# Decoder on one core: two of eight multiplications per expert tile moved from VectorE to ScalarE and GpSimd

## The chip, the cores and the metric

The kernel runs on one core of a Trainium2 chip. The metric is the device time of one execution in microseconds (us), over several runs of the same program. A core has TensorE (matmuls, PE in the profile; its weight loads are PEld), VectorE (DVE), ScalarE (ACT), GpSimd (POOL) and SyncE (SP). Each engine works through its own instruction list in order; semaphores tie the lists together.

## The reference

Two decoder layers over 16 x 256 tokens of width 256: causal attention, cross attention and a product-key expert layer (PEER), then banded attention, a BiDAF-like mix and a mixture of experts. Only the PEER layer is touched:

```python
q = (x @ Wq + bq).reshape(B, S, N_HEADS, D_QUERY)
s1 = einsum('bshd,nd->bshn', q1, K1); s2 = einsum('bshd,nd->bshn', q2, K2)
v1, i1 = top_k(s1, 10); v2, i2 = top_k(s2, 10)
vals, best = top_k(all pair sums, 10)
expert_idx = take_along_axis(i1 * 64 + i2, best)
scores = softmax(vals)
h = einsum('bsd,bshkd->bshk', x, W_down[expert_idx])
h = gelu(h) * scores
out = einsum('bshk,bshkd->bsd', h, W_up[expert_idx])
```

## The kernel before

The stages run one after another. `peer_stage` does 32 tiles of 128 tokens. It gathers nothing: all 4096 experts (32 groups `v` of 128) are computed densely, and a matrix of routing weights, zero where a token did not choose an expert, is multiplied in. A tile `t` is cut into eight chunks `n` of 16 tokens for the routing weights, and into eight quarters of four expert groups for the activations.

What one turn of the tile loop does on each engine, chunk by chunk (`macro` of each engine, in this order; nothing reorders it at run time):

- TensorE: `weights(t, n)` (L1000) makes the routing weights of 16 tokens with 48 small matmuls from one-hot matrices into one of two PSUM banks, `ps_w[:, n % 2]`. Called w(n) below. Between w(n) and w(n+1) stand `output(t-1)` (L1009, four expert groups of the tile before, from `g` and `up`) and `hidden(t+1)` (L990, the activations of four groups of the next tile into `ps_h`): out(n-1) and hid(n-1). For tile t+2, `turn_x` (L964) comes after w(1), `queries` (L971) after w(2), `scores` (L981) after w(3); `turn_uvw(t+1)` (L1018) comes after hid(4). Ahead of w(n), TensorE waits until the bank has been read, that is until the product of chunk n-2 is done.
- VectorE: for each n, `hots` (L1233, L1237) builds one-hot matrices two chunks ahead (`hot_e`, `hot_u`), then `weigh(n-1)` (L1245) multiplies `ps_w` into the 128x512 slice of `g`. The rest of the list is the choice of experts for later tiles: `best_eight`, `next_eight`, `places`, `lookup`, `choices` for t+1 and `halves` (L1258 to L1276) for t+2. The choice for t+1 ends in `uvw`, which TensorE turns (`turn_uvw`) and ScalarE takes (`take_uvw`, L1107 to L1109, semaphore `uvw_used`); `hots(t+1, 0)` at n = 6 waits for that.
- ScalarE: `gelu(t+1, n-1)` (L1087) after each hid(n-1), reading `ps_h` and writing `g`; at n = 1, 2, 3 it takes `xnT`, `qT` and `s` for tile t+2; at n = 2 `take_code`; at n = 3, behind `gelu(t+1, 2)`, `exps(t+1)` (L1093: a table load and eight small activations), at n = 5 `take_uvw`.
- GpSimd: `norm` (L1161) and `candidates` (L1175) at the tile's head, then `hots` (L1190): three 80x512 products `hot_v` from `hot_e` per chunk, two chunks ahead; `split` (L1154 to L1157) before those of chunk 0.

Of the kernel before, what the change touches and what calls it, by code (L numbers as in the profile page):

```python
# [6 lines left out]
P = 128  # L7
ALU = mybir.AluOpType
# [44 lines left out]
class Room:  # L53
# [12 lines left out]
    def sb(self, name, shape, dt=F32):  # L66
        return self.ctx.enter_context(self.nc.sbuf_tensor(f"{self.stage}_{name}", shape, dt))
# [4 lines left out]
    def sem(self, name):  # L72
        self.sems.append(self.nc.alloc_semaphore(f"{self.stage}_{name}"))
        return self.sems[-1]
# [751 lines left out]
EV = 32  # L826
CHUNK = 16
# [12 lines left out]
def peer_stage(nc, stats, ident, d):  # L840
# [6 lines left out]
    with ExitStack() as ctx:  # L847
        r = Room(nc, ctx, "peer")
        stats.open(r)
        sb, ps, sem = r.sb, r.ps, r.sem  # L850
        SEL = NQ * TOP
        wq = sb("wq", [P, DC, 2 * NQ * HALF])
        bq = sb("bq", [P, 4])
        keys = sb("keys", [P, 2 * KEYS])
# [33 lines left out]
        hot_v = sb("hot_v", [P, RING, 3, CHUNK // 2, EV, 2], BF16)  # L888
        g = sb("g", [P, 2, EV, P])
        mark = sb("mark", [P, 1])  # L890

        ps_q = ps("ps_q", [P, 512])
        ps_s = ps("ps_s", [P, 2, 512])
# [26 lines left out]
        v_ready = sem("v_ready")  # L920
        w_done = sem("w_done")
        gw_ready = sem("gw_ready")
        up_done = sem("up_done")
        x_used = sem("x_used")
        roots_ready = sem("roots_ready")
# [20 lines left out]
        def there(t):  # L946

            return not isinstance(t, int) or 0 <= t < TILES

        def by_pair(row, n):  # L950

# [3 lines left out]
        def _(pe):  # L955
# [38 lines left out]
            def weights(t, n):  # L994
                pe.wait_ge(u_ready, NCH * t + n + 1)
                pe.wait_ge(v_ready, NCH * t + n + 1)
                wait(pe, gw_ready, NCH * t + n - 1)
                for k in range(CHUNK):
                    for part in range(3):
                        mm = nc.tensor.matmul(ps_w[:, n % 2, k * EV:(k + 1) * EV], hot_u[0:SEL, n % RING, k // 2, :, k % 2],  # L1000
                                              hot_v[0:SEL, n % RING, part, k // 2, :, k % 2], start=(part == 0), stop=(part == 2))
                mm.then_inc(w_done, 1)

            def output(t, par, a, b):
                if a == 0:
                    pe.wait_ge(gw_ready, NCH * (t + 1))
                    wait(pe, x_used, t)
                for v in range(a, b):
                    mm = nc.tensor.matmul(ps_u[:], g[:, par, v, :], up[:, v, :], start=(v == 0), stop=(v == EV - 1))  # L1009
                if b == EV:  # L1010
                    mm.then_inc(up_done, 1)
# [51 lines left out]
        def _(act):  # L1063
# [20 lines left out]
            def gelu(t, par, n):  # L1084
# [2 lines left out]
                nc.scalar.activation(g[:, par, 4 * n:4 * n + 4, :].rearrange("p v s -> p (v s)"), ps_h[:, n % 2, :],  # L1087
                                     ACT.Gelu).then_inc(g_ready, 1)

            def exps(t):  # L1090
                act.wait_ge(exp_in, t + 1)
                for h in range(NQ):
                    ins = nc.scalar.activation(ew[:, h, :], ew[:, h, :], ACT.Exp, accum_out=es[:, h, :])  # L1093
                ins.then_inc(exp_out, 1)
# [28 lines left out]
            def macro(t, par):  # L1123
                for n in range(NCH):
                    if there(t + 2):
                        if n == 1:
                            take_x(t + 2, par)
                        if n == 2:
                            take_q(t + 2)
                        if n == 3:  # L1130
                            take_s(t + 2)
                    if there(t + 1):
                        if n == 2:
                            take_code(t + 1)
                        if n > 0:
                            gelu(t + 1, 1 - par, n - 1)
                        if n == 3:
                            exps(t + 1)
                        if n == 5:
                            take_uvw(t + 1, 1 - par)  # L1140
                if there(t + 1):
                    gelu(t + 1, 1 - par, NCH - 1)

# [3 lines left out]
        def _(pool):  # L1147
# [35 lines left out]
            def hots(t, par, n):  # L1183
# [6 lines left out]
                    ins = nc.gpsimd.tensor_tensor(hot_v[0:SEL, n % RING, part], hot_e[0:SEL, n % RING], w, ALU.mult)  # L1190
                ins.then_inc(v_ready, 1)

            def first():
                pool.wait_ge(roots_ready, 1)
                norm(0)
                norm(1)
                candidates(0)
                for n in range(AHEAD):
                    hots(0, 0, n)

            def macro(t, par):
                if there(t + 2):
                    norm(t + 2)
                if there(t + 1):
                    candidates(t + 1)
                for n in range(NCH):
                    if n < NCH - AHEAD:
                        hots(t, par, n + AHEAD)
                    elif there(t + 1):
                        hots(t + 1, 1 - par, n + AHEAD - NCH)  # L1210
                    if n == AGAIN:
                        steps.again()

# [3 lines left out]
        def _(dve):  # L1217
# [22 lines left out]
            def weigh(t, par, n):  # L1240
                if n == 0:
                    dve.wait_ge(g_ready, NCH * (t + 1))
                dve.wait_ge(w_done, NCH * t + n + 1)
                gs = g[:, par, :, n * CHUNK:(n + 1) * CHUNK]
                nc.vector.tensor_tensor(gs, ps_w[:, n % 2, :].rearrange("p (k v) -> p v k", v=EV), gs,  # L1245
                                        ALU.mult).then_inc(gw_ready, 1)
# [1059 lines left out]
```

## Time and profile before

| | us |
|---|---|
| three runs | 3786.21, 3789.82, 3791.73 (median 3789.82) |
| profiled execution, device time | 3788.22 |
| its span | 3786.4 |
| PEER stage, first to last product of `weigh` | 982.4 to 2473.6 |

| engine | busy of the span | busy of one steady PEER tile (47.41 us) |
|---|---|---|
| PE | 3288.4 (87%) | 44.00 |
| DVE | 2719.1 (72%) | 46.19 |
| ACT | 1203.2 (32%) | 12.61 |
| POOL | 2068.0 (55%) | 36.23 |

The profiled execution is 1.6 us below the median. A steady tile lasts from one `turn_x` to the next; the 28 that follow each other from 1030 to 2358 us are 47.1 to 47.6 us long. Busy shares are a mean over stages with different limits, so the last column is what counts for a change inside PEER. An engine's position in its instruction list matters too: it can be idle in one place of the tile and late in another.

### The profile page before, as it was taken

The numbers are of one execution on the slowest core, as the hardware profiler recorded it, in microseconds if no ns is written. First come the engines' busy times: TensorE is split into PE (matmuls) and PEld (weight loads), VectorE is DVE, ScalarE is ACT, GpSimd is POOL, SyncE is SP. The second block draws the span as 40 slices with busy tenths as digits, with TensorE's granted clock in tenths as the row PEclk, the third lists the DMA queues.
The fourth block names the chain that finished last, engine by engine and source line by source line (L and its number), as shares of the span: only waits on it lengthen the run. The fifth ranks groups of instructions, "written<-read, shape, count | busy, mean of one in ns | idle before, by whom it ended". The sixth has DMA issues, their size and how long they took to land. (4 is left out here: it accounts for less than half of the span.)

```text
span 3786.4 us, 93267 instructions
## 1 busy us (share of the span) xinstructions
PE 3288.4 (87%) x33694; PEld 2790.3 (74%) x33695; DVE 2719.1 (72%) x10688; ACT 1203.2 (32%) x3140; POOL 2068.0 (55%) x2392
## 2 busy tenths in 40 slices
PE   6999957786599999999999999978888897699998
PEld 4777735554488888888888888855564687699998
DVE  6666634554999999999999999948887554533333
ACT  1443435552222222222222222225664221122221
POOL 4444335551677777777777777858885000233333
PEclk8999978997799999999999999989999896799999
DMA  5444434443000000000000000034453115466665
GB/s 152 110 108 110 109 83 116 123 113 122 1 2 2 2 2 2 2 2 2 2 2 2 2 2 2 2 91 124 125 130 74 34 33 160 123 181 183 182 182 136
DMA packets 256114, 277.90 MB, mean 73 GB/s; under 512 B 44001, under 2 KB 200673, under 8 KB 255201
## 3 DMA queue, kind: packets, MB, share of 16 engines
q1 hardware_dynamic: 242081, 253.69, 23.5%
q0 software_dynamic: 13632, 18.91, 3.3%
q8 instruction: 245, 4.01, 0.4%
q14 instruction: 156, 1.28, 0.1%
HBM read 187.63 MB, written 72.29 MB: 69 GB/s over the span
## 5 line engine op out<-in xcount | busy, mean ns | idle before, releaser
L1190 POOL TENSOR_TENSOR peer_hot_v<-peer_hot_e,peer_parts 80x512 bf16<-80x512 bf16 x768 | 990.9, 1316 | 320.9 <-DVE peer_hot_e L1233 311.7
L1009 PE MATMUL peer_ps_u<-peer_up,peer_g 128*128 128x256 f32 x2048 | 534.3, 408 | 0.6 <-DVE x_all L1331 0.6
L990 PEld LDWEIGHTS peer_ps_h<-peer_xnT,peer_down 128*128 128x128 f32 x4096 | 512.7, 197 | 15.7 <-DMA peer_down<-in_peer_down 0.9
L990 PE MATMUL peer_ps_h<-peer_xnT,peer_down 128*128 128x128 f32 x4096 | 512.3, 280 | 0.6 <-DMA peer_down<-in_peer_down 0.6
L1000 PE MATMUL peer_ps_w<-peer_hot_v,peer_hot_u 80*128 80x32 bf16 x12288 | 347.3, 177 | 145.4 <-DVE peer_g L1245 97.5
L1000 PEld LDWEIGHTS peer_ps_w<-peer_hot_v,peer_hot_u 80*128 80x128 bf16 x12288 | 337.0, 97 | 167.3 <-issue 92.1
L1009 PEld LDWEIGHTS peer_ps_u<-peer_up,peer_g 128*128 128x128 f32 x2048 | 393.1, 202 | 53.5 <-issue 1.0
L1087 ACT ACTIVATE peer_g<-peer_ps_h 128x512 f32<-128x512 f32 x256 | 152.9, 597 | 840.5 <-PE peer_ps_h L990 840.2
L1237 DVE TENSOR_TENSOR peer_hot_u<-peer_count,peer_uvT 80x2048 bf16<-80x2048 bf16 x256 | 349.4, 1365 | 0.0
L2072 POOL DMA_INDIRECT out<-moe_y,moe_target x71 | 112.6, 1585 | 312.6 <-DVE moe_y L2203 309.6
L2007 PE MATMUL moe_ps_t<-moe_xgT,moe_w 128*128 128x128 f32 x2272 | 267.3, 276 | 0.0
L2066 POOL DMA_INDIRECT moe_xg<-moe_xn_rows,moe_source x71 | 70.2, 988 | 357.2 <-DVE moe_target L2173 325.0
L2007 PEld LDWEIGHTS moe_ps_t<-moe_xgT,moe_w 128*128 128x128 f32 x2272 | 261.5, 193 | 0.1
L2017 PE MATMUL moe_ps_y<-moe_w,moe_hT 128*128 x1136 | 256.8, 379 | 0.0
L2017 PEld LDWEIGHTS moe_ps_y<-moe_w,moe_hT 128*128 128x128 f32 x1136 | 210.5, 190 | 25.7
L772 DVE TENSOR_REDUCE band_nmax<-band_ps 128x2 f32<-128x512 f32 x256 | 171.3, 680 | 42.4 <-PE band_ps L511 42.1
L769 DVE TENSOR_REDUCE causal_nmax<-causal_ps 128x1 f32<-128x128 f32 (+1 forms) x512 | 153.2, 349 | 58.1 <-PE causal_ps L515 57.7
L634 ACT ACTIVATE causal_probT<-causal_ps 128x384 f32<-128x384 f32 x256 | 124.7, 489 | 202.4 <-PE causal_ps L538 199.4
L1245 DVE TENSOR_TENSOR peer_g<-peer_ps_w,peer_g 128x512 f32<-128x512 f32 x256 | 173.8, 679 | 7.4 <-PE peer_ps_w L1000 7.4
L2203 DVE SCALAR_TENSOR_TENSOR moe_y<-moe_ps_y,moe_gate,moe_b2w 128x256 f32<-128x256 f32 x71 | 34.4, 484 | 194.9 <-PE moe_ps_y L2017 194.9
L634 ACT ACTIVATE band_probT<-band_ps 128x512 f32<-128x512 f32 x256 | 147.2, 594 | 62.1 <-PE band_ps L535 57.7
L772 DVE TENSOR_REDUCE cross_nmax<-cross_ps 128x2 f32<-128x240 f32 x256 | 97.8, 400 | 96.0 <-PE cross_ps L511 95.0
(362 smaller groups left out, 7073.9 us busy)
## 6 DMA issues: line engine op xcount, KB each, us to landing
moe_w<-in_moe_w SPq DMA_DIRECT2D x142, 512.0 KB
causal_qs<-causal_qscratch SPq DMA_DIRECT2D x32, 384.0 KB, 3.9
cross_qs<-cross_qscratch SPq DMA_DIRECT2D x32, 384.0 KB, 3.6
band_qs<-band_qscratch SPq DMA_DIRECT2D x32, 384.0 KB, 4.1
moe_w<-in_moe_w SPq DMA_DIRECT2D x8, 1024.0 KB, 11.7
causal_qscratch<-causal_part SPq DMA_DIRECT2D x32, 192.0 KB, 2.6
causal_kscratch<-causal_part SPq DMA_DIRECT2D x32, 192.0 KB, 2.0
causal_ks<-causal_kscratch SPq DMA_DIRECT2D x32, 192.0 KB, 4.2
```

The source lines that it names most:

```text
L634: nc.scalar.activation(probT[0:KN, h, :], ps_2[0:KN, h % 2, 0:COLS], ACT.Exp).then_inc(p_ready, 1)
L769: ins = nc.vector.tensor_reduce(nmax[:, q, h:h + 1], ps_1[:, h % 2, qcol[q]:qcol[q] + seen[q]], AX.X, ALU.max, negate=True)
L772: ins = nc.vector.tensor_reduce(nmax[:, :, h], ps_1[:, h % 2, 0:TT * KS].rearrange("p (q k) -> p q k", q=TT), AX.X, ALU.max, negate=True)
L990: mm = nc.tensor.matmul(ps_h[:, n % 2, k * P:(k + 1) * P], down[:, c, 4 * n + k, :], xnT[:, par, c, :], start=(c == 0), stop=(c == DC - 1))
L1000: mm = nc.tensor.matmul(ps_w[:, n % 2, k * EV:(k + 1) * EV], hot_u[0:SEL, n % RING, k // 2, :, k % 2], hot_v[0:SEL, n % RING, part, k // 2 ...
L1009: mm = nc.tensor.matmul(ps_u[:], g[:, par, v, :], up[:, v, :], start=(v == 0), stop=(v == EV - 1))
L1087: nc.scalar.activation(g[:, par, 4 * n:4 * n + 4, :].rearrange("p v s -> p (v s)"), ps_h[:, n % 2, :], ACT.Gelu).then_inc(g_ready, 1)
L1190: ins = nc.gpsimd.tensor_tensor(hot_v[0:SEL, n % RING, part], hot_e[0:SEL, n % RING], w, ALU.mult)
L1237: nc.vector.tensor_tensor(hot_u[0:SEL, n % RING], numbers.broadcast_to((SEL, CHUNK // 2, P, 2)), ut, ALU.is_equal).then_inc(u_ready, 1)
L1245: nc.vector.tensor_tensor(gs, ps_w[:, n % 2, :].rearrange("p (k v) -> p v k", v=EV), gs, ALU.mult).then_inc(gw_ready, 1)
L2007: mm = nc.tensor.matmul(ps_h[:, half, m * P:(m + 1) * P], w1[:, par, half, c, m * P:(m + 1) * P], xgT[:, par, c, :], start=(c == 0), stop= ...
L2017: mm = nc.tensor.matmul(ps_y[:, par, 0:D], hT[:, par, m, :], w2[:, ex, m, :], start=(m == 0), stop=(m == HC - 1))
```

## The change

Chunks 2 and 5 of each tile (`APART`) are no longer multiplied by VectorE. ScalarE copies the bank `ps_w[:, n % 2]` into a new SBUF buffer `wcopy` (`take_w`, one 128x512 activation), and GpSimd multiplies `wcopy` into the slice of `g` (its own `weigh`, one 128x512 `tensor_tensor`, that reads `wcopy` at a stride of 32 elements). Two semaphores are new: `w_copied` (ScalarE's copy has been made) and `gp_ready` (GpSimd's product has been made). TensorE's wait ahead of w(n) is now `w_free`: for n = 4 and n = 7 on `w_copied`, else on `gw_ready`, whose count is six per tile. `output` waits for both kinds of products before its first matmul of a tile.

```diff
+        APART = (2, 5)
+        HERE = NCH - len(APART)
...
+        def w_free(eng, t, n):
+            if n < 0:
+                t, n = t - 1, n + NCH
+            if t < 0:
+                return
+            if n in APART:
+                eng.wait_ge(w_copied, len(APART) * t + APART.index(n) + 1)
+            else:
+                eng.wait_ge(gw_ready, HERE * t + n + 1 - sum(k < n for k in APART))
...
             def weights(t, n):
-                wait(pe, gw_ready, NCH * t + n - 1)
+                w_free(pe, t, n - 2)
...
             def output(t, par, a, b):
                 if a == 0:
-                    pe.wait_ge(gw_ready, NCH * (t + 1))
+                    pe.wait_ge(gw_ready, HERE * (t + 1))
+                    pe.wait_ge(gp_ready, len(APART) * (t + 1))
...
+            def take_w(t, n):                                  # ScalarE
+                k = APART.index(n)
+                act.wait_ge(w_done, NCH * t + n + 1)
+                wait(act, gp_ready, len(APART) * (t - 1) + k + 1)
+                nc.scalar.activation(wcopy[:, k, :], ps_w[:, n % 2, :], ACT.Copy).then_inc(w_copied, 1)
...
                         if n == 5:
                             take_uvw(t + 1, 1 - par)
+                    if n - 1 in APART:
+                        take_w(t, n - 1)
...
+            def weigh(t, par, n):                              # GpSimd
+                k = APART.index(n)
+                pool.wait_ge(w_copied, len(APART) * t + k + 1)
+                gs = g[:, par, :, n * CHUNK:(n + 1) * CHUNK]
+                nc.gpsimd.tensor_tensor(gs, wcopy[:, k, :].rearrange("p (k v) -> p v k", v=EV), gs, ALU.mult).then_inc(gp_ready, 1)
...
                     elif there(t + 1):
                         hots(t + 1, 1 - par, n + AHEAD - NCH)
+                    if n - 2 in APART:
+                        weigh(t, par, n - 2)
...
             def weigh(t, par, n):                              # VectorE
                 if n == 0:
                     dve.wait_ge(g_ready, NCH * (t + 1))
+                if n in APART:
+                    return
```

ScalarE's list in a steady tile before, from `s` of tile t+2 to the last `gelu` but one. `peer_g<-peer_ps_h` is a `gelu`, `peer_ew` are the exponentials:

```order
L1081 ACTIVATE peer_s<-peer_ps_s 128x1024
L1087 ACTIVATE peer_g<-peer_ps_h 128x512
L1093 ACT_TABLE_LOAD
L1093 ACTIVATE peer_ew,peer_es<-peer_ew 128x10 x8
L1087 ACT_TABLE_LOAD
L1087 ACTIVATE peer_g<-peer_ps_h 128x512 x2
L1107 ACTIVATE peer_uvT<-peer_ps_q 80x256
L1108 ACTIVATE peer_parts<-peer_ps_q 80x128
L1109 ACTIVATE peer_wT<-peer_ps_q 80x128
L1087 ACTIVATE peer_g<-peer_ps_h 128x512 x3
```

The same piece of ScalarE's list in the changed kernel, with the copies as `peer_wcopy`:

```order
L1098 ACTIVATE peer_s<-peer_ps_s 128x1024
L1104 ACTIVATE peer_g<-peer_ps_h 128x512
L1116 ACT_TABLE_LOAD
L1116 ACTIVATE peer_ew,peer_es<-peer_ew 128x10 x8
L1111 ACTIVATE peer_wcopy<-peer_ps_w 128x512
L1104 ACT_TABLE_LOAD
L1104 ACTIVATE peer_g<-peer_ps_h 128x512 x2
L1130 ACTIVATE peer_uvT<-peer_ps_q 80x256
L1131 ACTIVATE peer_parts<-peer_ps_q 80x128
L1132 ACTIVATE peer_wT<-peer_ps_q 80x128
L1104 ACTIVATE peer_g<-peer_ps_h 128x512
L1111 ACTIVATE peer_wcopy<-peer_ps_w 128x512
```

The copy of chunk 2 stands behind the exponentials and ahead of the second table load; that of chunk 5 stands behind `gelu(t+1, 5)`.

GpSimd's list before, from the `hot_v` products of a tile to the head of the next:

```order
L1190 TENSOR_TENSOR peer_hot_v<-peer_hot_e,peer_parts 80x512 x9
L1154 TENSOR_TENSOR peer_rest<-peer_wT,peer_parts 80x128
L1155 CAST peer_parts<-peer_rest 80x128
L1156 TENSOR_TENSOR peer_rest<-peer_rest,peer_parts 80x128
L1157 CAST peer_parts<-peer_rest 80x128
L1190 TENSOR_TENSOR peer_hot_v<-peer_hot_e,peer_parts 80x512 x6
L1161 TENSOR_SCALAR peer_xn<-x_all,mean,rstd 128x256
```

The same piece in the changed kernel:

```order
L1215 TENSOR_TENSOR peer_hot_v<-peer_hot_e,peer_parts 80x512 x6
L1222 TENSOR_TENSOR peer_g<-peer_wcopy,peer_g 128x32x16
L1215 TENSOR_TENSOR peer_hot_v<-peer_hot_e,peer_parts 80x512 x3
L1179 TENSOR_TENSOR peer_rest<-peer_wT,peer_parts 80x128
L1180 CAST peer_parts<-peer_rest 80x128
L1181 TENSOR_TENSOR peer_rest<-peer_rest,peer_parts 80x128
L1182 CAST peer_parts<-peer_rest 80x128
L1215 TENSOR_TENSOR peer_hot_v<-peer_hot_e,peer_parts 80x512 x6
L1222 TENSOR_TENSOR peer_g<-peer_wcopy,peer_g 128x32x16
L1186 TENSOR_SCALAR peer_xn<-x_all,mean,rstd 128x256
```

The product of chunk 2 stands between the `hot_v` of chunks 6 and 7, that of chunk 5 between the `hot_v` of the next tile's chunk 1 and `norm`. On TensorE no instruction moves, only what w(4) and w(7) wait for; on VectorE the products of chunks 2 and 5 are gone and nothing else moves.

## Rows read from the trace of the kernel before

**Rows 1.** Windows: us, busy (count) of PE, PEld, DVE, ACT, POOL; PEclk; DMA

```profile
1741.58:1788.99 47.41, 44.00 (x620) 41.13 (x616) 46.19 (x235) 12.61 (x36) 36.23 (x35) 0.97 0.01 2
1030.00:2358.00 1328.00, 1226.44 (x17155) 1148.99 (x17151) 1293.82 (x6552) 353.16 (x1008) 1018.31 (x954) 0.97 0.01 2
1741.40:1744.80 3.40, 3.40 (x22) 2.86 (x19) 3.40 (x4) 0.38 (x1) 3.40 (x3) 0.50 0.00 0
```

**Rows 2.** Timeline of PE in one steady tile: start, us, group

```profile
1740.37 1.37 PE L1000 MATMUL peer_ps_w<-peer_hot_v,peer_hot_u 80*128 80x32 bf16 x48 [0.96 <-DVE peer_g L1245]
...
1742.04 3.27 PE L1009 MATMUL peer_ps_u<-peer_up,peer_g 128*128 128x256 f32 x8
1745.14 1.95 PE L990 MATMUL peer_ps_h<-peer_xnT,peer_down 128*128 128x128 f32 x16
...
1750.00 1.89 PE L1009 MATMUL peer_ps_u<-peer_up,peer_g 128*128 128x256 f32 x8
1751.73 1.95 PE L990 MATMUL peer_ps_h<-peer_xnT,peer_down 128*128 128x128 f32 x16
...
1757.72 1.95 PE L990 MATMUL peer_ps_h<-peer_xnT,peer_down 128*128 128x128 f32 x16
1759.50 1.36 PE L1000 MATMUL peer_ps_w<-peer_hot_v,peer_hot_u 80*128 80x32 bf16 x48
...
1765.71 1.35 PE L1000 MATMUL peer_ps_w<-peer_hot_v,peer_hot_u 80*128 80x32 bf16 x48 [1.24 <-DVE peer_g L1245]
...
1770.50 0.49 PE L1018 MATMUL peer_ps_q<-ident,peer_uvw 128*80 128x128 f32 x3
1771.22 1.35 PE L1000 MATMUL peer_ps_w<-peer_hot_v,peer_hot_u 80*128 80x32 bf16 x48 [0.23 <-DVE peer_g L1245]
...
1774.23 1.95 PE L990 MATMUL peer_ps_h<-peer_xnT,peer_down 128*128 128x128 f32 x16
1777.16 1.35 PE L1000 MATMUL peer_ps_w<-peer_hot_v,peer_hot_u 80*128 80x32 bf16 x48 [0.98 <-DVE peer_g L1245]
...
1787.79 1.35 PE L1000 MATMUL peer_ps_w<-peer_hot_v,peer_hot_u 80*128 80x32 bf16 x48 [0.96 <-DVE peer_g L1245]
```

**Rows 3.** Timeline of ACT in the same tile

```profile
1759.70 0.60 ACT L1087 ACTIVATE peer_g<-peer_ps_h 128x512 f32<-128x512 f32 x1 [2.67 <-PE peer_ps_h L990]
1760.32 1.28 ACT L1093 ACT_TABLE_LOAD   x1
...
1763.08 0.19 ACT L1093 ACTIVATION_READ_ACCUMULATOR peer_ew<-peer_ew 128x1 f32 x1
...
1771.62 0.28 ACT L1109 ACTIVATE peer_wT<-peer_ps_q 80x128 f32<-80x128 f32 x1
```

**Rows 4.** Timeline of DVE in the same tile

```profile
1757.07 0.68 DVE L1245 TENSOR_TENSOR peer_g<-peer_ps_w,peer_g 128x512 f32<-128x512 f32 x1
1757.69 0.06 DVE L1258 MEMSET peer_mark<- 128x1 f32 x1
...
1774.86 0.42 DVE L1233 TENSOR_TENSOR peer_hot_e<-peer_count,peer_uvT 80x512 bf16<-80x512 bf16 x1
...
1786.96 0.68 DVE L1245 TENSOR_TENSOR peer_g<-peer_ps_w,peer_g 128x512 f32<-128x512 f32 x1
```

**Rows 5.** Timeline of PE in the stage's first tile

```profile
1006.79 1.39 PE L1000 MATMUL peer_ps_w<-peer_hot_v,peer_hot_u 80*128 80x32 bf16 x48 [3.32 <-DVE peer_g L1245]
1008.02 3.42 PE L990 MATMUL peer_ps_h<-peer_xnT,peer_down 128*128 128x128 f32 x16
```

**Rows 6.** POOL, lines view: count, busy us, mean ns, idle before

```profile
L690 POOL TENSOR_TENSOR x_all<-x_all,band_bo 128x512 f32<-128x512 f32 x16 | 20.2, 1260 | 1.7 <-DVE band_xn L729 1.7
```

**Rows 7.** Timeline of POOL in the same tile

```profile
1742.46 7.21 POOL L1190 TENSOR_TENSOR peer_hot_v<-peer_hot_e,peer_parts 80x512 bf16<-80x512 bf16 x6
...
1785.24 1.22 POOL L1161 TENSOR_SCALAR peer_xn<-x_all,mean,rstd 128x256 f32<-128x256 f32 x1
```

**Rows 8.** Line view of `hot_u`: ns of one, least/median/most, first and last start

```profile
L1237 DVE TENSOR_TENSOR peer_hot_u<-peer_count,peer_uvT x256: 1207/1215/2058, 971.7 to 2462.2; 80x2048 bf16<-80x2048 bf16 x128
```

More of the change, by code:

```diff
@@ L890, in peer_stage @@
         mark = sb("mark", [P, 1])
+        wcopy = sb("wcopy", [P, len(APART), 512])
         ps_q = ps("ps_q", [P, 512])
@@ L922, in peer_stage @@
         gw_ready = sem("gw_ready")
+        w_copied = sem("w_copied")
+        gp_ready = sem("gp_ready")
         up_done = sem("up_done")
```

## The prediction

> **What bounds the kernel now.** I read the page for busy shares by slice (PEER is where DVE stands at nine tenths), then the windows view on one steady tile [rows 1], then the timelines of the engines in that tile [rows 2 to 4, 7]. The windows say that VectorE is the fullest: 46.19 of 47.41 us. What it leaves open are the short gaps ahead of linked steps. The timeline of PE says the same from the other side: PE waits for `peer_g L1245`, VectorE's product, ahead of w(5), w(6), w(7) and w(1), for 1.24, 0.23, 0.98 and 0.96 us [rows 2]. So the tile's length is VectorE's list, and PE has slack of some 3.9 us in it: the 3.41 us of those waits, and 0.17 us for three of them, because a group that isn't held starts 0.17 us ahead of the modelled end of the one before it (hid(2) starts at 1757.72, lasts 1.95, and w(4) starts at 1759.50 [rows 2]). PE has a second reserve: its clock is down to 0.50, the lower of its two levels (1.2 GHz), for 3.40 us at the tile's head [rows 1], where out(0) takes 3.10 us to the next group against 1.73 us for out(1) [rows 2]. Together PE's own work is about 47.4 - 3.9 - 1.4 = 42.1 us.
>
> That slack is spread: none of it lies between w(1) and w(4). From 1740.37 to the end of hid(2) at 1759.67 PE works without a wait.
>
> **Part 1: what VectorE loses.** Two of its eight products. One takes 0.68 us busy, but the next instruction starts 0.62 us after it (1757.07 to 1757.69 [rows 4]), so 2 x 0.62 = 1.24 us per tile. Were VectorE still the bound, that would be 31 x 1.24 = 38 us.
>
> **Part 2: the two copies on ScalarE.** They are not on the trace. Nearest row: `gelu`, also 128x512 from PSUM to SBUF, 0.60 us [rows 3]. ScalarE is busy for 12.61 us of the tile, so its load doesn't matter. Its order does. The copy of chunk 2 stands behind gelu(2), the table load and the exponentials. gelu(2) starts when hid(2) is done (1759.70), the load at 1760.32, the last exponential's accumulator read ends at 1763.27 [rows 3]. The copy then ends at 1763.9, and PE gets the semaphore 0.15 us later: 1764.05. PE issues w(4) at 1759.50 now, right behind hid(2); from now on w(4) needs this copy, because the bank of w(4) is that of w(2). Everything behind w(4) in PE's list waits too: out(3), hid(3), w(5), and the turning of `uvw`. And hid(2) is itself on PE's list directly ahead of w(4), so starting earlier doesn't help: PE does nothing from the end of hid(2) until four steps of ScalarE are through. Bounds of this wait: at least 0.60 + 1.28 + 1.66 + 0.60 = 4.1 us, at most 5.7 if the copy needed a table load of its own (the changed list has none there, so I take 4.4).
>
> Lateness of PE against the tile before, following [rows 2]: at w(4) 1764.05 - 1759.50 = 4.55. The wait ahead of w(5) goes (VectorE has long made product 3): 4.55 - 1.41 = 3.14. Ahead of w(6): 3.14 - 0.23 = 2.91. Ahead of w(7) the new wait is the copy of chunk 5: it stands behind gelu(5), and that behind hid(5). hid(5) ends, 0.04, gelu 0.60, 0.02, copy 0.60, 0.15 semaphore = 1.41 us of idleness, where there are 0.98 now: 2.91 + 0.43 = 3.34. Ahead of the next w(1) the wait of 0.96 + 0.15 goes: 3.34 - 1.11 = 2.23. So a PE that loses nothing else comes round 2.23 us later than now: its loop, 42.1 us of work plus waits of 4.55 and 1.58 and the clock loss, has become longer than VectorE's 46.2 us.
>
> **Part 3: the clock.** The tile's head has w(0), a wait of 0.96, w(1): there the clock falls today. With product 7 long made, that wait is gone and PE runs through the place, so I expect most of that loss (1.37 us) to go. In its stead PE stands still for 4.4 us ahead of w(4). In the stage's first tile a wait of 3.32 us ahead of a w was followed by a hid of 3.42 us in place of 1.95 [rows 5, 2], a loss of 1.47. I take one such loss per tile: 2.23 - 1.37 + 1.47 = 2.3 us per tile. Bounds: no loss at all, 2.23 - 1.37 = 0.86; both losses, 2.23 + 1.47 = 3.7.
>
> **Part 4: what VectorE meets.** Its `hots(t+1, 0)` waits for `uvw_used`. The turning of `uvw` starts at 1770.50 and ScalarE's last copy of it ends at 1771.90, 1.40 later [rows 2, 3]. With PE 3.14 us late this becomes 1775.04; VectorE, freed of one product, arrives at 1774.86 - 0.62 = 1774.24 [rows 4] and waits 0.8 us. It has product 7 done at about 1787.2, and PE asks for it, for the next w(1), at 1790.0. So VectorE waits, PE does not wait for it, and the 1.24 us are worth nothing.
>
> **Part 5: GpSimd.** Two multiplications of 128x512 f32 with both inputs in SBUF: a contiguous one takes 1.26 us [rows 6], and nothing on the trace excludes less for this form, since only its reads differ. This one reads `wcopy` 128 bytes apart, so I take 1.7, with 1.2 and 2.5 as ends, the latter twice the contiguous row. The Trainium skill (GPSIMD Engine Reference, Performance pitfalls for Q7 kernels) says that a read with a step over 8 bytes costs about 2.9 instead of 1.9 cycles per element; that would be an estimate of 1.9 us for the whole instruction, no run here shows it, and the sum would stay as it is. GpSimd is busy 36.2 us of the tile, 39.6 then. The product of chunk 5 pushes `norm` (now at 1785.24) and `candidates` and the `hot_v` of the next chunk 2 back by about 1.7 - 0.6 = 1.1 us. That `hot_v` ends 3.6 us after 1742.46 [rows 7], 0.9 ahead of the w(2) that needs it, and PE is 2.2 late: hidden, up to some 2.5 us a product. Product 2 delays the `hot_v` of chunk 7, with over 3 us to spare before w(7).
>
> **The sum.** The profiled execution has 3788.2 us around a span of 3786.4. 30 of 32 tiles have the whole pattern: 30 x 2.3 = 69. The first tile (no `output`, PE mostly idle) and the last (no exponentials) may keep their 1.24 each: -2. 3788.2 + 67 = 3855; the median of the runs shown is 1.6 higher than the profiled one, within the rounding of this. I say 3854.
>
> **The rivals.**
>
> *PE waits but the clock stays up.* 0.86 x 30 - 2 = +24: 3812. For it: the wait ends before w(4), whose 48 small matmuls are the work least in need of the clock, and part of the slow stretch may fall into the idle time itself. Against: [rows 5]. Chance 0.16.
>
> *Both clock losses,* one kept at the head, one new, 3.7 x 30 - 2 = +109: 3897. For it: w(7) with 1.4 us of waiting ahead of it is another thin place. Chance 0.14.
>
> *VectorE stays the bound, and the kernel is faster.* Place: w(4). If PE's two new waits together stayed under 46.2 - 42.1 = 4.1 us, against the 6.1 worked out here, the tile would be VectorE's 46.2 us: 3788.2 - 38 = 3750. For it: VectorE has 97% of the tile, PE has slack, the copies are small. It needs the exponentials to be out of the copy's way, and the order of ScalarE's list and the start of gelu(2) behind hid(2) [rows 3] say they aren't. Between 4.1 and 5.3 us of waits it would be a smaller gain, above that a loss. Chance 0.07 for faster, 0.05 for a balance within 0.2%.
>
> *The port.* One `hot_u` took 2058 ns against a median of 1215 [rows 8], while GpSimd was at its three `hot_v`. If each new product of GpSimd holds a VectorE instruction up for its whole 1.7 us, VectorE's list is 46.2 + 3.4 = 49.6 us, +2.2 x 30 - 2: 3852. The Trainium skill (SBUF - State Buffer, Who interferes with whom) has the rule: a VectorE instruction with two SBUF inputs contends with a GpSimd instruction that reads SBUF, and the one that comes first keeps the port. By that rule the moved product costs VectorE more than it saves. Against it: product 5 runs while VectorE searches maxima, and VectorE has 0.8 us to wait anyway. It comes to the same time by another way; chance 0.04 as the bound.
>
> **How the numbers follow.** Forecast 0.54, its own range 3835 to 3875; with the port 0.58; 0.16 at 3812; 0.14 at 3897; balance 0.05; faster 0.07. Range 3798 to 3897, which leaves out the balance, the gain and half of the highest case. Faster by over 0.2% (7.6 us, about what a measurement of this kernel can tell from none) 0.07, within 0.05, slower 0.88.
>
> **What would show it.** The new rows: `wcopy` x64 at about 0.60 us; between the table load of L1116 and that of L1104 in each tile. PE's wait ahead of w(4) named after ScalarE's copy, 4.4 us, 31 times; ahead of w(7) 1.4; those for VectorE's product almost gone. `turn_x` to `turn_x` about 49.7 us. VectorE idle for `wT` ahead of `hot_e`. The granted clock of 0.50 behind w(4) and not at the head. I am wrong if turn_x to turn_x is under 47.4, or if PE's wait ahead of w(4) is under 3 us.

## The result and the profile after

The changed kernel takes 3891.22 us in the median of four runs (3881.8 to 3897.67), the kernel before 3788.80 beside it (four runs): a ratio of 1.0268, interval 1.0243 to 1.0293. That is 102 us more, where 66 were forecast: the time is inside the range of 3798 to 3897, near its upper end. The profiled execution took 3881.8 us, its span is 3880.0.

The windows view of the changed kernel, over most of PEER, over one tile and over 4.85 us behind that tile's w(4), with the columns of [rows 1]:

```profile
1035.00:2450.00 1415.00, 1255.61 (x17053) 1173.18 (x17050) 1329.84 (x6479) 378.77 (x1062) 1099.26 (x1005) 0.92 0.01 2
1747.31:1797.16 49.85, 44.36 (x620) 41.66 (x616) 45.87 (x231) 13.57 (x38) 37.31 (x36) 0.93 0.01 2
1768.05:1772.90 4.85, 4.85 (x57) 4.13 (x58) 4.68 (x21) 1.15 (x1) 4.79 (x4) 0.50 0.00 0
```

VectorE was busy 46.19 of 47.41 us of a tile [rows 1]; now it is 45.87 of 49.85, so it has 4 us left over, and the mean granted clock fell from 0.97 to 0.92. The tile's length is no longer VectorE's. From `turn_x` to `turn_x` the 26 tiles from 1087.32 to 2404.91 us last 50.68 us in the mean (49.05 to 52.47), against 47.4 before. 3.2 us over 30 tiles are 97 us; the two spans differ by 93.6.

The timeline of PE in that tile and at two places of the next (start, length, group, and in brackets the wait ahead of it), which answers to [rows 2]:

```profile
1761.87 1.95 PE L1006 MATMUL peer_ps_h<-peer_xnT,peer_down 128*128 128x128 f32 x16
1768.05 1.44 PE L1016 MATMUL peer_ps_w<-peer_hot_v,peer_hot_u 80*128 80x32 bf16 x48 [4.23 <-ACT peer_wcopy L1111]
1769.33 3.76 PE L1026 MATMUL peer_ps_u<-peer_up,peer_g 128*128 128x256 f32 x8
1772.88 2.37 PE L1006 MATMUL peer_ps_h<-peer_xnT,peer_down 128*128 128x128 f32 x16
1775.09 1.36 PE L1016 MATMUL peer_ps_w<-peer_hot_v,peer_hot_u 80*128 80x32 bf16 x48
...
1783.23 1.95 PE L1006 MATMUL peer_ps_h<-peer_xnT,peer_down 128*128 128x128 f32 x16
1786.45 1.35 PE L1016 MATMUL peer_ps_w<-peer_hot_v,peer_hot_u 80*128 80x32 bf16 x48 [1.27 <-ACT peer_wcopy L1111]
...
1794.75 2.56 PE L1016 MATMUL peer_ps_w<-peer_hot_v,peer_hot_u 80*128 80x32 bf16 x96
1797.16 0.42 PE L980 MATMUL peer_ps_q<-ident,peer_xn 128*128 128x128 f32 x2
...
1801.46 1.35 PE L1016 MATMUL peer_ps_w<-peer_hot_v,peer_hot_u 80*128 80x32 bf16 x48 [0.36 <-POOL peer_hot_v L1215]
...
1838.41 3.59 PE L1026 MATMUL peer_ps_u<-peer_up,peer_g 128*128 128x256 f32 x8
```

Four things stand in these rows. The waits for VectorE ahead of w(5), w(6), w(7) and w(1) are gone; w(0) and w(1) are now one group of 96. In their place stand 4.23 us ahead of w(4) and 1.27 us ahead of w(7), both for ScalarE's copy. Behind w(4), out(3) takes 3.76 us in place of 1.97: PE is at the lower of its two clock levels (0.50, 1.2 GHz), where it was at the full one before the wait. And in the next tile the same happens once more, behind w(7) (1838.41).

ScalarE in the same tile, which answers to [rows 3]:

```profile
1763.86 0.60 ACT L1104 ACTIVATE peer_g<-peer_ps_h 128x512 f32<-128x512 f32 x1 [2.67 <-PE peer_ps_h L1006]
1764.47 1.28 ACT L1116 ACT_TABLE_LOAD   x1
...
1767.23 0.19 ACT L1116 ACTIVATION_READ_ACCUMULATOR peer_ew<-peer_ew 128x1 f32 x1
1767.33 0.57 ACT L1111 ACTIVATE peer_wcopy<-peer_ps_w 128x512 f32<-128x512 f32 x1
1767.92 1.28 ACT L1104 ACT_TABLE_LOAD   x1
```

This is the chain of the prediction, row by row: gelu(2), table load, exponentials, copy, and then w(4) at 1768.05. The copy needs no table load of its own. The waits view of 1035 to 2450 us (us in total, times, longest) says that it is so in every tile, and that others wait as well:

```profile
PE peer_ps_w L1016 <- ACT peer_wcopy L1111: 153.8, 56, 4.2
...
POOL peer_rest L1179 <- ACT peer_wT L1132: 74.2, 28, 3.3
...
DVE peer_hot_e L1266 <- issue: 28.3, 17, 1.9
```

Now VectorE. Its groups by form (count, busy us, mean ns of one), of the kernel before from 1030 to 2358 us:

```profile
L1233 DVE TENSOR_TENSOR peer_hot_e<-peer_count,peer_uvT 80x512 bf16<-80x512 bf16 x224 | 113.4, 506 | 4.8
L1302 DVE TENSOR_TENSOR peer_eq<-peer_count,peer_tpf 128x2240 f16<-128x2240 bf16 x28 | 37.9, 1353 | 1.0
L1310 DVE TENSOR_TENSOR peer_eq<-peer_eq,peer_code 128x2240 f16<-128x2240 f16 x28 | 37.1, 1325 | 1.0
L1321 DVE TENSOR_TENSOR peer_uvw<-peer_ew,peer_er 128x80 f32<-128x80 f32 x28 | 6.8, 242 | 1.0
```

and of the changed kernel from 1035 to 2400 us, where the same instructions are at L1266, L1337, L1345 and L1356:

```profile
L1266 DVE TENSOR_TENSOR peer_hot_e<-peer_count,peer_uvT 80x512 bf16<-80x512 bf16 x215 | 125.5, 584 | 36.0 <-issue 26.5 <-DVE peer_besti L1306 5.6
L1345 DVE TENSOR_TENSOR peer_eq<-peer_eq,peer_code 128x2240 f16<-128x2240 f16 x27 | 43.3, 1604 | 0.9
L1356 DVE TENSOR_TENSOR peer_uvw<-peer_ew,peer_er 128x80 f32<-128x80 f32 x27 | 40.8, 1511 | 0.9
L1337 DVE TENSOR_TENSOR peer_eq<-peer_count,peer_tpf 128x2240 f16<-128x2240 bf16 x27 | 40.4, 1495 | 0.9
```

A product of 128x80, the smallest of the list, went from 242 to 1511 ns. The timelines of GpSimd and VectorE in the tile say what lies beside it:

```profile
1771.35 1.49 POOL L1222 TENSOR_TENSOR peer_g<-peer_wcopy,peer_g 128x512 f32<-128x512 f32 x1
...
1791.49 1.53 POOL L1222 TENSOR_TENSOR peer_g<-peer_wcopy,peer_g 128x512 f32<-128x512 f32 x1
```

```profile
1771.44 1.50 DVE L1356 TENSOR_TENSOR peer_uvw<-peer_ew,peer_er 128x80 f32<-128x80 f32 x1
...
1789.15 0.59 DVE L1295 MAX8 peer_ranks<-peer_s 128x8 f32<-128x64 f32 x4
...
1791.45 0.61 DVE L1303 MAX8 peer_ranks<-peer_s 128x8 f32<-128x64 f32 x4
...
1794.51 1.65 DVE L1266 TENSOR_TENSOR peer_hot_e<-peer_count,peer_uvT 80x512 bf16<-80x512 bf16 x1
```

GpSimd's product of chunk 2 starts 0.09 us ahead of VectorE's `uvw`, which takes 0.24 us alone and ends here 0.10 us behind the product's end (1772.94 and 1772.84). The product of chunk 5 runs beside `MAX8`, whose only input is 128x64, and costs it nothing (0.61 us, as the same `MAX8` takes in the kernel before). Of the 1.24 us that VectorE gave away per tile, its stretched instructions take back 1.27 for `uvw`, 0.28 and 0.14 for the two `eq` and 8 x 0.08 = 0.62 for `hot_e`: 2.3 us. The Trainium skill (SBUF — State Buffer, Who interferes with whom) has the rule: "A DVE instruction with two SBUF inputs contends with a GpSimd instruction that reads SBUF". The rows agree, with the whole remainder of GpSimd's instruction as its price.

### The profile page after: what moved, and what is told of

Read it like the earlier page. It is cut to its first block and busy times, and to the rows that moved or that the text cites. A ratio compares the mean times of both kernels' runs of the same rounds, so it can differ in the third digit from the quotient of the medians.

```text
span 3880.0 us, 93394 instructions
## 1 busy us (share of the span) xinstructions
PE 3320.2 (86%) x33694; PEld 2817.7 (73%) x33695; DVE 2754.8 (71%) x10624; ACT 1232.9 (32%) x3204; POOL 2164.4 (56%) x2456
## 3 DMA queue, kind: packets, MB, share of 16 engines
q14 instruction: 156, 1.28, 0.1%
## 5 line engine op out<-in xcount | busy, mean ns | idle before, releaser
L1215 POOL TENSOR_TENSOR peer_hot_v<-peer_hot_e,peer_parts 80x512 bf16<-80x512 bf16 x768 | 962.0, 1279 | 271.5 <-DVE peer_hot_e L1266 268.7
L1026 PE MATMUL peer_ps_u<-peer_up,peer_g 128*128 128x256 f32 x2048 | 566.2, 426 | 0.6 <-DVE x_all L1366 0.6
L1006 PEld LDWEIGHTS peer_ps_h<-peer_xnT,peer_down 128*128 128x128 f32 x4096 | 522.3, 200 | 19.1 <-DMA peer_down<-in_peer_down 2.1
L1016 PE MATMUL peer_ps_w<-peer_hot_v,peer_hot_u 80*128 80x32 bf16 x12288 | 345.5, 178 | 209.9 <-ACT peer_wcopy L1111 170.2
L1016 PEld LDWEIGHTS peer_ps_w<-peer_hot_v,peer_hot_u 80*128 80x128 bf16 x12288 | 337.9, 98 | 227.8 <-issue 220.2
L1026 PEld LDWEIGHTS peer_ps_u<-peer_up,peer_g 128*128 128x128 f32 x2048 | 411.8, 211 | 59.9 <-issue 1.0
L1266 DVE TENSOR_TENSOR peer_hot_e<-peer_count,peer_uvT 80x512 bf16<-80x512 bf16 x256 | 149.9, 585 | 42.7 <-issue 30.0
```

What stands on the lines that cost most here:

```text
L1006: mm = nc.tensor.matmul(ps_h[:, n % 2, k * P:(k + 1) * P], down[:, c, 4 * n + k, :], xnT[:, par, c, :], start=(c == 0), stop=(c == DC - 1))
L1266: nc.vector.tensor_tensor(hot_e[0:SEL, n % RING], numbers[:, :, 0:EV, :].broadcast_to((SEL, CHUNK // 2, EV, 2)), vt, ALU.is_equal).then_in ...
```

## The experiments

The question was how the 102 us are made up: of PE's waits for copies, of the clock behind them, and of GpSimd's product. Each difference is against the kernel before as it ran beside that kernel: its medians are 3788.80 us for the changed kernel and 3786.67, 3792.26 and 3786.78 us in the three sets of experiments.

| kernel | median us | against before | ratio and interval |
|---|---|---|---|
| changed kernel | 3891.22 | +102.4 | 1.0268 (1.0243 to 1.0293) |
| both copies earlier | 3834.10 | +47.4 | 1.0134 (1.0116 to 1.0152) |
| PE kept busy ahead of w(4) | 3836.43 | +49.8 | 1.0129 (1.0112 to 1.0146) |
| chunk 5 alone, copy late | 3796.05 | +9.4 | 1.0025 (1.0015 to 1.0035) |
| chunk 2 alone, copy late | 3869.85 | +77.6 | 1.0200 (1.0182 to 1.0219) |
| VectorE multiplies from the copy | 4081.90 | +295.2 | 1.0781 (1.0763 to 1.0799) |
| short product, copies late | 3866.84 | +74.6 | 1.0199 (1.0184 to 1.0215) |
| short product, copies earlier | 3770.27 | -22.0 | 0.9941 (0.9925 to 0.9957) |
| copies earlier, products ahead of `hot_v` | 3822.37 | +30.1 | 1.0080 (1.0067 to 1.0094) |
| copies earlier, products at two other places | 3820.58 | +33.8 | 1.0085 (1.0071 to 1.0099) |
| chunk 5 alone, copy earlier, product ahead of `hot_v` | 3784.83 | -2.0 | 0.9992 (0.9982 to 1.0001) |

### Both copies earlier

The copy stands at the head of ScalarE's turn instead of at its end: ahead of gelu(n-1) and of the exponentials. All else is as in the changed kernel.

```diff
                 for n in range(NCH):
+                    if n - 1 in APART:
+                        take_w(t, n - 1)
                     if there(t + 2):
...
-                    if n - 1 in APART:
-                        take_w(t, n - 1)
```

> Both copies of ScalarE are moved to the head of their chunk's turn: the copy of chunk 2 ahead of the taking of s, gelu(2) and the exponentials, that of chunk 5 ahead of gelu(5). The rest is the changed kernel. Theory (order of ScalarE's list): PE's waits ahead of w(4) and w(7) for the copy are gone, with them the clock loss behind them; VectorE is the bound again with two products less, 47.45 - 1.24 = 46.2 us per tile: about 3750. Rival (the port: GpSimd's products hold VectorE up by more than they save): the tile stays above 47.45 us, 3790 or more.

Half of it held: no wait of PE for a copy is left, and +102.4 became +47.4. But it is not the 3750 us that VectorE's shorter list would give. The timeline of PE and of GpSimd in two of its tiles, and of VectorE beside them:

```profile
1775.32 1.35 PE L1016 MATMUL peer_ps_w<-peer_hot_v,peer_hot_u 80*128 80x32 bf16 x48 [2.10 <-issue]
```

```profile
1768.25 3.97 POOL L1200 TENSOR_TENSOR peer_cand<-peer_ranks 128x160 f32<-128x160 f32 x5
1772.18 10.21 POOL L1215 TENSOR_TENSOR peer_hot_v<-peer_hot_e,peer_parts 80x512 bf16<-80x512 bf16 x9
...
1797.25 1.51 POOL L1222 TENSOR_TENSOR peer_g<-peer_wcopy,peer_g 128x512 f32<-128x512 f32 x1
```

```profile
1797.33 1.52 DVE L1356 TENSOR_TENSOR peer_uvw<-peer_ew,peer_er 128x80 f32<-128x80 f32 x1
```

`uvw` is held for the whole product again. At the tile's head GpSimd is late by the other product: its `candidates` reach to 1772.2 and the `hot_v` behind them start late, so that w(2) stands still for 2.10 us. So the order theory explains 55 of the 102 us, and the rest hangs on GpSimd's product.

### PE kept busy ahead of w(4)

Eight matmuls whose result nobody reads stand ahead of PE's wait for w(4). They wait until gelu(1) has read the bank that they write.

```diff
             def weights(t, n):
+                if n == 4 and there(t + 1):
+                    pe.wait_ge(g_ready, NCH * (t + 1) + 2)
+                    for k in range(8):
+                        nc.tensor.matmul(ps_h[:, 1, 0:D], down[:, 0, k, :], up[:, k, :], start=True, stop=True)
                 w_free(pe, t, n - 2)
```

> The changed kernel with eight extra f32 matmuls of 128x256 on PE ahead of its wait for w(4), into a bank that nobody reads then; they take about 3.5 us of the 4.2 us that PE waits there. Theory (the clock accounts for what the wait itself doesn't): the granted clock stays at its upper level behind w(4), out(3) takes 1.8 us instead of 3.5, the tile is 47.8 us plus what w(7) loses: 3805 to 3840. Rival (the waits alone, or something else that slows the groups behind w(4)): no gain, 3880 or more.

As expected: -52.6 us against the changed kernel, with nothing shortened but the idle time. The timeline of PE (L1016 is the added group here, L1020 is w, L1030 is out) and the window of the added group and the wait:

```profile
1785.24 3.62 PE L1016 MATMUL peer_ps_h<-peer_up,peer_down 128*128 128x256 f32 x16
1789.54 1.37 PE L1020 MATMUL peer_ps_w<-peer_hot_v,peer_hot_u 80*128 80x32 bf16 x48 [0.68 <-ACT peer_wcopy L1115]
1790.76 1.97 PE L1030 MATMUL peer_ps_u<-peer_up,peer_g 128*128 128x256 f32 x8
```

```profile
1785.24:1789.54 4.30, 3.62 (x19) 2.86 (x17) 4.16 (x6) 4.06 (x20) 0.55 (x2) 1.00 0.00 0
```

PE still gets w(4) no sooner than the copy lets it, but out(3) behind it takes 1.97 us, not 3.76, and the granted clock stays at its full level (2.4 GHz). Of 27 tiles 15 last 47.5 to 48.7 us; the other 12 last 50.5 to 51.2, 10 of them with the low clock behind w(7). So of the 102 us some 53 go with the low clock behind w(4), which costs 2.2 us per tile, 66 us in all, by the ledger further down; they don't all come off, since other limits come next. This is, but for w(7), the rival "PE waits but the clock stays up", made on purpose. It comes to 3836 and not to 3812: the window of 1035 to 2440 us has VectorE busy for 1364.85 of 1405.00 us, so its list with the stretched instructions (`uvw` 1549 ns) is nearly the bound again. PE waits for up to 1.77 us ahead of w(2), and the losses behind w(7) come on top:

```profile
1035.00:2440.00 1405.00, 1326.21 (x17952) 1238.05 (x17951) 1364.85 (x6596) 389.72 (x1093) 1123.24 (x1024) 0.99 0.01 2
```

### Chunk 5 alone, and chunk 2 alone

```diff
-        APART = (2, 5)
+        APART = (5,)
```

> Only chunk 5 leaves VectorE, with the copy at the changed kernel's place (behind gelu(5)). Theory (order): the wait ahead of w(7) is 1.3 us where it was 1.0, PE's slack covers it, VectorE stays the bound with one product less: 3789 - 31 x 0.62 = 3770. Rival (port): GpSimd's product costs VectorE more than 0.62 us, 3789 or more.

```diff
-        APART = (2, 5)
+        APART = (2,)
```

> Only chunk 2 leaves VectorE, with the copy at the changed kernel's place, behind the exponentials. Theory: PE waits 4.2 us ahead of w(4) in each tile and loses the clock behind it for two stretches; w(7) waits for VectorE as before. Tile about 49 us, 3830 to 3850. Rival (both waits are needed to pass VectorE's list): under 3800.

Chunk 5 costs 9.4 us where 17 us of gain were expected; chunk 2 costs 77.6, more than the 40 to 60 expected. The waits view of the second, 1035 to 2440 us:

```profile
PE peer_ps_w L1016 <- ACT peer_wcopy L1111: 118.3, 28, 4.2
PE peer_ps_w L1016 <- issue: 37.0, 27, 1.4
```

4.2 us in each tile, so the wait ahead of w(4) and the clock loss behind it hang on chunk 2, and its product holds `uvw` (1515 ns) as in the changed kernel. What the expectation of 49 us a tile lacked is the second row: 1.4 us in each tile ahead of w(2). There PE waits for GpSimd, since w(2) starts at 1737.15, 0.16 us behind the end of its `hot_v`. The kernel before has such a wait of 1.3 us in some tiles only (15.2 us in 12 of them), so by these rows the tile is 50.05 us. How much of this wait is due to the product isn't separated. With chunk 5 alone there is no such wait (1.3 us at most) and `uvw` takes 242 ns, but `eq` of L1337 goes to 1589 ns and `hot_e` to 564. That is 0.24 + 8 x 0.06 = 0.7 us against the 0.62 that the product took off VectorE; with `hot_u` (1355 for 1342 ns) and the cast of `ranks` (272 for 196) it is 0.9 us, so some 8 of the 9.4 us. The two kernels with one chunk cost 87 us together, the changed kernel 102; what the missing 15 are isn't settled.

### VectorE multiplies from the copy

Meant as a control for GpSimd's part: the two products go back to VectorE, but read the copy; GpSimd has none.

```diff
                 if n in APART:
-                    return
+                    k = APART.index(n)
+                    dve.wait_ge(w_copied, len(APART) * t + k + 1)
+                    gs = g[:, par, :, n * CHUNK:(n + 1) * CHUNK]
+                    nc.vector.tensor_tensor(gs, wcopy[:, k, :].rearrange("p (k v) -> p v k", v=EV), gs,
+                                            ALU.mult).then_inc(gp_ready, 1)
```

> ScalarE copies at the places of the changed kernel, but VectorE multiplies from the copy, at its old place in its list, and GpSimd has no product. Theory (order): PE's loop is untouched by who multiplies, tiles of 49 to 52.5 us as in the changed kernel: 3880 to 3895. Rival (port): without GpSimd's products the loss goes, 3790.

It is not the control it was meant to be. The waits view of 1035 to 2440 us:

```profile
DVE peer_g L1278 <- ACT peer_wcopy L1111: 205.7, 49, 7.3
PE peer_ps_w L1016 <- ACT peer_wcopy L1111: 136.0, 49, 4.2
```

VectorE, the engine without slack, now waits for the late copy itself, up to 7.3 us at a time. Neither time that was expected came. It shows what a wait costs when it stands in the list of the bounding engine (+295 us). On GpSimd it shows one thing: without its products `uvw` takes 242 ns, `hot_e` 506 and the two `eq` 1357 and 1325, as in the kernel before, so the stretched instructions go with them. VectorE's own product from the copy isn't cheap either: 1406 ns in the mean and 1.09 us where GpSimd is idle (1803.90), against 679 ns from PSUM.

### A short product on GpSimd

GpSimd multiplies 16 columns instead of 512, which takes 0.22 us. The weights of the other columns of chunks 2 and 5 are left out of the computation in these two kernels. First with the copies early, then in the changed kernel's order.

```diff
-                nc.gpsimd.tensor_tensor(gs, wcopy[:, k, :].rearrange("p (k v) -> p v k", v=EV), gs, ALU.mult).then_inc(gp_ready, 1)
+                few = wcopy[:, k, :].rearrange("p (k v) -> p v k", v=EV)[:, 0:1, :]
+                nc.gpsimd.tensor_tensor(gs[:, 0:1, :], few, gs[:, 0:1, :], ALU.mult).then_inc(gp_ready, 1)
```

> copy_first, with GpSimd's product cut to 16 of 512 columns (the weights of the other columns of chunks 2 and 5 are left out). Theory (port): VectorE is no longer held up: 46.2 us per tile, 3750. Rival (something else in copy_first, such as the copies' place on ScalarE, keeps it slow): 3820 or more.

> The changed kernel, with GpSimd's product cut to 16 of 512 columns (the weights of the other columns of chunks 2 and 5 are left out). Theory (PE's two waits and the clock are the bound, the port is hidden behind them): 3870 to 3890, as the changed kernel. Rival (the port is the cause): 3800 or less.

With early copies this is the only kernel faster than before, by 22 us. The groups of VectorE, 1035 to 2400 us:

```profile
L1346 DVE TENSOR_TENSOR peer_eq<-peer_eq,peer_code 128x2240 f16<-128x2240 f16 x29 | 50.4, 1737 | 1.0
...
L1357 DVE TENSOR_TENSOR peer_uvw<-peer_ew,peer_er 128x80 f32<-128x80 f32 x29 | 7.0, 241 | 1.0
```

`uvw` is back at 241 ns. It stays short of the 3750 us expected in part because one `eq` now takes 1737 ns instead of 1325: in the shifted order it starts at 1521.80, before GpSimd's last `hot_v` ends at 1522.37. That is 0.41 of the 1.24 us that VectorE gained, 12 of the 20 us missing. The pairs of runs price the product: 47.4 + 22.0 = 69 us where VectorE is close to the bound, and 102.4 - 74.6 = 28 us in the changed kernel, where PE is (the two profiled spans, 3880.0 and 3863.6, differ by 16 only). In those two traces the tile is 50.68 and 50.06 us: 0.2 of the 0.6 us are PE's wait for `hot_v` ahead of w(2), which is gone, and the rest is clock, since 9 of 27 tiles have the short loss of 1.1 us now and 4 had it before. Why the pattern of the low clock changes with the product isn't settled. And the pairs price the order of the copies without any product: 74.6 + 22.0 = 97 us. The two costs overlap, since either engine's delay hides part of the other's.

### Where the product would stand better

Three kernels, all with early copies, move GpSimd's products to other places of its list. First, both ahead of the `hot_v` of their turn:

```diff
+                    if n - 2 in APART:
+                        weigh(t, par, n - 2)
                     if n < NCH - AHEAD:
                         hots(t, par, n + AHEAD)
...
-                    if n - 2 in APART:
-                        weigh(t, par, n - 2)
```

> copy_first, with GpSimd's two products moved ahead of the hot_v of the same turn: that of chunk 2 ahead of hot_v(6), that of chunk 5 ahead of hot_v(1) of the next tile, where GpSimd waits for hot_e now and VectorE searches maxima, with one SBUF input. Theory (port, by place): the uvw product of VectorE falls from 1522 back to 242 ns, the two eq products to about 1350 and 1325, norm and candidates come in time; VectorE's list is 46.2 us: 3750 to 3765. Rival (GpSimd's added load hurts wherever it stands): 3800 or more.

Then product 2 behind the `hot_v` of chunk 7 and product 5 ahead of the `hot_v` of the next chunk 1:

```diff
+                    if n == 7:
+                        weigh(t, par, 5)
                     if n < NCH - AHEAD:
                         hots(t, par, n + AHEAD)
...
-                    if n - 2 in APART:
-                        weigh(t, par, n - 2)
+                    if n == 5:
+                        weigh(t, par, 2)
```

> copy_first, with both of GpSimd's products at places where VectorE searches maxima: that of chunk 2 behind hot_v(7), at n = 5, that of chunk 5 ahead of hot_v(1) of the next tile, at n = 7. Theory (what a product costs is decided by the VectorE instruction that it meets): the uvw product takes 242 ns, the eq products 1325 to 1734 and 742, hot_e some 560; VectorE's list is 46.2 + 0.4 + 0.5 = 47.1 us or less, 3770 to 3785. Rival (two products never fit into GpSimd's list without making hot_v, norm or candidates late): 3800 or more.

And product 5 at that place alone, with chunk 2 left to VectorE:

```diff
-        APART = (2, 5)
+        APART = (5,)
...
+                    if n - 2 in APART:
+                        weigh(t, par, n - 2)
                     if n < NCH - AHEAD:
                         hots(t, par, n + AHEAD)
```

> Only chunk 5 leaves VectorE; its copy is ahead of gelu(5), its product ahead of hot_v(1) of the next tile. Theory: one product less on VectorE, 0.62 us, against at most 0.5 us on hot_e and no wait of PE for a copy: 3770 to 3785. Rival (the port takes back what one product saves): 3789 or more.

The first two are slower than before, +30 and +34 us, the third is no different (-2.0 us). VectorE's groups in the first of them, 1035 to 2400 us:

```profile
L1345 DVE TENSOR_TENSOR peer_eq<-peer_eq,peer_code 128x2240 f16<-128x2240 f16 x28 | 51.1, 1824 | 1.0
L1347 DVE TENSOR_TENSOR peer_eq<-peer_eq 128x1120 f16<-128x1120 f16 x28 | 50.7, 1810 | 1.0
...
L1356 DVE TENSOR_TENSOR peer_uvw<-peer_ew,peer_er 128x80 f32<-128x80 f32 x28 | 6.8, 241 | 1.0
```

`uvw` is free (241 ns), and two instructions of `lookup` are held in its place: 1824 ns for 1325, and 1810 for 742, which the second takes in the kernel before and in all the other ones. One tile shows by what:

```profile
1774.59 1.75 DVE L1345 TENSOR_TENSOR peer_eq<-peer_eq,peer_code 128x2240 f16<-128x2240 f16 x1
1776.37 1.94 DVE L1347 TENSOR_TENSOR peer_eq<-peer_eq 128x1120 f16<-128x1120 f16 x1
```

```profile
1775.12 2.59 POOL L1222 TENSOR_TENSOR peer_g<-peer_wcopy,peer_g 128x512 f32<-128x512 f32 x1
```

The first is held by the last `hot_v`, which ends at 1775.15, as with the short product; only the second is held by the product, which ends at 1777.71. And the product, which started 0.53 us behind VectorE's first `eq`, takes 2.59 us in place of 1.5: here GpSimd is the one that is held. In the kernel with products at two other places `hot_e` is what is met:

```profile
L1268 DVE TENSOR_TENSOR peer_hot_e<-peer_count,peer_uvT 80x512 bf16<-80x512 bf16 x227 | 159.4, 702 | 4.8
```

and less so in the one with chunk 5 alone:

```profile
L1266 DVE TENSOR_TENSOR peer_hot_e<-peer_count,peer_uvT 80x512 bf16<-80x512 bf16 x231 | 129.9, 562 | 4.9
```

That is 702 and 562 ns, against 506 before. The five kernels with early copies come near to one sum, VectorE's list (us per tile; the last column is the measured difference over 30 tiles):

| kernel | products given away | `uvw` | `eq` | `hot_e`, 8 of them | sum | measured |
|---|---|---|---|---|---|---|
| both copies earlier | -1.24 | +1.28 | +0.43 | +0.46 | +0.93 | +1.58 |
| products ahead of `hot_v` | -1.24 | 0 | +1.57 | +0.54 | +0.87 | +1.00 |
| two other places | -1.24 | 0 | +0.34 | +1.57 | +0.67 | +1.13 |
| chunk 5 alone, early | -0.62 | 0 | 0 | +0.45 | -0.17 | -0.07 |
| short product, early | -1.24 | 0 | +0.41 | -0.02 | -0.85 | -0.73 |

The signs agree, and the order but for the second and third, whose measured intervals overlap; sizes agree within 0.1 to 0.7 us. What the first and third are above the sum isn't settled; the first has waits of PE such as the 2.10 us ahead of w(2), too. In every kernel with a whole product some VectorE instruction with two inputs from SBUF was stretched. In the kernel before, GpSimd's two longest gaps in the tile (2.11 us up to 1756.09 and 3.85 up to 1763.90) lie beside the two `eq`; a place beside the searches alone, with nothing behind it moved onto something else, wasn't found, and no version with the whole computation beat the kernel before.

## Why the prediction was right in its sign and short in its size

**Bound and Part 1.** Right that VectorE's list bounded the kernel before and that it would cease to. The short product with early copies shows that its 1.24 us are real where nothing takes them back: -22 us of the 38 worked out.

**Part 2, the copies.** Right, step by step. The copy took 592 ns in the median (0.60 taken), needed no table load, and the wait ahead of w(4) is 4.23 us (4.4), ahead of w(7) 1.27 (1.41). From the end of hid(2) and hid(5) by the pace of PE's groups the waits are 4.40 and 1.44 us, 5.84 together, where I had 6.13.

**Part 3, the clock: the step that was mis-sized.** That the loss at the tile's head would go is right: w(0) and w(1) run through, with the clock up. That one loss of 1.47 us would come behind w(4) is half of it. In the tile shown, out(3) lasts 3.55 us up to the next group instead of 1.80, hid(3) 2.21 instead of 1.79, w(4) 1.28 instead of 1.20: 2.25 us. In the next tile hid(3) is longer still, which makes it 2.6, and behind w(7) out takes 3.38 instead of 1.80, with its neighbour 1.7 us more. Of the 27 tiles from 1087 us on, 10 have this second loss behind w(7), and 4 have the short form behind w(4), where the wait and w(4) are followed by an out(3) of 2.98 us and all else is at full pace: 1.1 us. The mean is (13 x 2.25 + 10 x 4.3 + 4 x 1.1) / 27 = 2.8 us, not 1.47. The bound "both losses" (3.7 per tile) paired the loss behind w(4) with one at the head that is gone; its place was w(7), which I had named only as a remark for the rival, while I had sized the loss by the stage's first tile [rows 5], a single hid behind a wait of 3.32 us, where out(3) comes first here and the low clock reaches over two groups.

The ledger of a tile by these rows: PE's own work 41.8 (42.1 expected), waits 5.84, clock 2.8, `hot_v` 0.2, together 50.6; measured 50.68. Against my 2.3 us: clock +1.4, waits -0.3, work -0.3, `hot_v` +0.2, which makes 3.3 (3.2 measured). The clock term alone carries the miss; keeping PE busy through the wait took 53 us off. (The sum itself gives 3855 for the profiled execution and 3857 with the 1.6 us that it names; I wrote 3854.)

**Part 4.** Right in kind: VectorE waits for `uvw_used` ahead of `hot_e`, 28.3 us in 17 of the tiles (17 x 1.7), and GpSimd for `wT`, 74.2 us. VectorE's gain was worth nothing there, as said. With the product shortened, VectorE's wait grows to 70.7 us in 28 places, the time that its stretched `uvw` had filled before.

**Part 5 and the rival "port": priced too low.** The duration was between the ends: 1.51 us, not 1.7. (The estimate by the Trainium skill, GPSIMD Engine Reference, Performance pitfalls for Q7 kernels, 1.9 us, was too high too; the strided form costs 1.51 against 1.26 us for the contiguous one [rows 6].) "Hidden" was wrong by 28 us in the medians and 16 in the profiled pair. Product 2 holds `uvw`, product 5 pushes `norm` and `candidates` into VectorE's `hot_e` (1.65 us at 1794.51 in place of 0.56 for the same one before), and then PE waits for `hot_v` ahead of w(2) in some tiles (0.36 us at 1801.46), just where I had counted 0.9 us in reserve. That wait is 0.2 us per tile, some 6 us; the rest shows as clock losses and its path isn't settled. The rival had the right mechanism and looked only at product 5, which does run beside the searches and holds nothing. I had not asked what lies beside product 2. As the bound alone it would not have come to 3852 but to the +47 us of the kernel with early copies, 3834.

**The other rivals.** VectorE did not stay the bound: PE's two waits are 5.84 us, above the 4.1 up to which it would have.

**The range** held because its upper end was the case with two clock losses. That is in part luck: that case had its second loss at the head and in every tile, and the runs have it behind w(7) and in 10 of 27.

## What to carry to other kernels

Before work is moved off the fullest engine, look up in the trace what stands ahead of the hand-over on the helping engine's list, since PE, when it waits for it, pays twice: for the wait of 4.2 us and for the lower clock behind it, 2.25 us in the tile shown. GpSimd is no free helper for VectorE: here each product with inputs in SBUF took 0.62 us off VectorE's list, and with what it pushed back it made VectorE's other instructions 0.45 to 1.2 us longer, so list which instructions will lie beside it at its new place and at the places of all that it pushes back. A shortened form of the added instruction, left where it is, prices it, but the instructions behind it move as well.

## What the runs showed of the hardware that I had not expected

- A VectorE product of 128x80 takes 0.24 us by itself and 1.50 us when it starts 0.09 us behind a GpSimd product of 1.49 us, and it ends 0.10 us behind it. What it pays goes by what is left of GpSimd's instruction and not by its own size: 1.26 us where 1.40 were left, and 1.20 for one of 128x1120 where 1.34 were left. It goes the other way too: a GpSimd product that started 0.53 us behind a VectorE instruction took 2.59 us in place of 1.5.
- After 4.2 us of idleness PE ran at the lower of its two clock levels through out(3) and part of hid(3): 2.25 to 2.6 us were lost in most tiles, against 1.47 behind 3.3 us of idleness in the stage's first tile [rows 5], where less work follows at once. Matmuls whose result nobody reads, put into the idle time, kept the full level (granted 1.00) and took 53 us off the kernel.
- The same idleness of 1.27 us ahead of w(7) is followed by the low clock in 10 of 27 tiles and not in the others. What decides it in one tile isn't settled; the pattern repeats every two to four tiles.
